# A product that nobody reads, issued before each chunk's sum in the message passes and in the attention pass

## The reference, cut to what matters

```
src, dst = edge_index                       # 31875 edges, sorted by dst
def _gine(x, ...):                          # called 4 times
    e = edge_attr @ eW + eb
    m = relu(x[src] + e)
    agg = segment_sum(m, dst, num_segments=N)
    h = (1.0 + eps) * x + agg
    return relu(h @ W1 + b1) @ W2 + b2
...
# attention: h_src = h_all[edge_type, src]
w = exp(leaky(scores) - amax[dst])
msg = h_src * (w / denom[dst])
out = segment_sum(msg, dst, num_segments=n)
```

## Time and profile before

| | us |
|---|---|
| median of 3 runs | 4661.29 (4660.78 to 4661.66) |
| the profiled execution | 4685.71 |
| its span, first to last instruction | 4684.1 |
| gathers of the first message pass, first to last issue | 180.1 to 567.7 |
| gathers of the second | 653.1 to 1043.0 |
| gathers of the third | 1131.0 to 1518.7 |
| gathers of the fourth | 1605.7 to 1993.6 |
| gathers of the attention pass | 2709.7 to 3092.9 |

### The profile page before, as it was taken

How to read it: one execution, slowest core, us unless ns; L and a number is a source line. 1 busy time by engine, 2 the same in 40 slices (tenths; PEclk the granted TensorE clock), 3 DMA queues, 4 the chain that set the end, 5 groups by cost and what they waited for, 6 DMA issues and landing times. The chain is left out here.

```text
span 4684.1 us, 57224 instructions
## 1 busy us (share of the span) xinstructions
PE 2923.7 (62%) x16851; PEld 2401.0 (51%) x16852; DVE 2212.2 (47%) x5663; ACT 867.9 (19%) x2228; POOL 1871.3 (40%) x1982
## 2 busy tenths in 40 slices
PE   3566746664666566642568626665949639947392
PEld 3455535553555355522556413335938639936382
DVE  6655645554555555564243437681064421134113
ACT  1122312221222122210112100001300103310020
POOL 4366546664666466624323467731010020020212
PEclk7788878777887778875678657676979859978696
DMA  6633323332333233303312133315947449945594
GB/s 157 217 89 89 78 65 89 88 83 59 89 90 88 57 87 89 89 15 124 100 55 74 28 82 93 92 41 190 304 145 240 150 159 328 325 150 174 181 333 128
DMA packets 357397, 598.97 MB, mean 128 GB/s; under 512 B 81862, under 2 KB 239864, under 8 KB 354808
## 3 DMA queue, kind: packets, MB, share of 16 engines
q1 hardware_dynamic: 245816, 357.76, 23.3%
q0 software_dynamic: 88640, 214.25, 16.3%
q10 hardware_dynamic: 22656, 23.54, 1.5%
HBM read 499.63 MB, written 95.75 MB: 127 GB/s over the span
## 5 line engine op out<-in xcount | busy, mean ns | idle before, releaser
L833 POOL DMA_INDIRECT gine_got<-gine_table,src x1056 | 1024.5, 970 | 619.7 <-issue 251.1
L893 PE MATMUL gine_p_sum<-gine_hot,gine_got 128*128 128x128 f32 x4224 | 846.2, 334 | 565.1 <-DVE stack_acc L930 200.1
L893 PEld LDWEIGHTS gine_p_sum<-gine_hot,gine_got 128*128 128x128 f32 x4224 | 707.4, 238 | 719.0 <-issue 648.6
L922 DVE TENSOR_TENSOR gine_got<-gine_got,gine_p_edge 128x256 f32<-128x256 f32 x1056 | 440.2, 418 | 633.5 <-PE gine_p_edge L884 365.0
L901 ACT ACTIVATE gine_got<-gine_got 128x256 f32<-128x256 f32 x1056 | 439.0, 417 | 1201.1 <-issue 750.5
L488 POOL DMA_INDIRECT adjacency<-value,place x264 | 281.1, 1065 | 475.9 <-POOLq L54 166.2
L930 DVE TENSOR_TENSOR stack_acc<-stack_acc,gine_p_sum 128x256 f32 x1056 | 438.9, 416 | 3.5 <-issue 0.7
L883 PE MATMUL gine_p_edge<-gine_w_a,edge_space 128*128 128x256 bf16 x1056 | 338.3, 320 | 42.6 <-issue 34.7
L1368 PE MATMUL ffn_p_h<-ffn_xt,ffn_w 128*128 128x128 f32 x2864 | 347.3, 279 | 1.1 <-DMA ffn_w<-in_L_ffn_w 0.7
L1368 PEld LDWEIGHTS ffn_p_h<-ffn_xt,ffn_w 128*128 128x128 f32 x2864 | 337.3, 196 | 3.8 <-DMA ffn_w<-in_L_ffn_w 2.6
L884 PE MATMUL gine_p_edge<-gine_w_b,edge_space 128*128 128x256 bf16 x1056 | 336.8, 319 | 0.0
(11 more groups left out here) (398 smaller groups left out, 3526.2 us busy)
## 6 DMA issues: line engine op xcount, KB each, us to landing
gcn_a<-adjacency SPq DMA_DIRECT2D x270, 320.0 KB
ffn_w<-in_L_ffn_W SPq DMA_DIRECT2D x74, 1024.0 KB
ffn_w<-in_L_ffn_w SPq DMA_DIRECT2D x60, 1024.0 KB
ffn_w<-in_L_ffn_w SPq DMA_DIRECT2D x90, 512.0 KB
adjacency<-zero_row ACTq DMA_DIRECT2D x3, 7200.0 KB, 43.8
gine_got<-gine_table,src POOLq DMA_INDIRECT x1056
h_table<-score_rows SPq DMA_DIRECT2D x15, 1056.0 KB
adjacency<-zero_row SPq DMA_DIRECT2D x1, 7200.0 KB, 28.1
```

Of the source, the lines that this page charges most:

```text
L833: pool.indirect_dma_start(got[:, c % RING, :], None, table, bass.IndirectOffsetOnAxis(ap=rows[:, c:c + 1], axis=0)).then_inc(gathered[c % ...
L893: ins = nc.tensor.matmul(p_sum[d % 4][:, half * P:(half + 1) * P], got[:, d % RING, half * P:(half + 1) * P], hot[:, d % HOTS, :], start=T ...
L922: nc.vector.tensor_tensor(got[:, c % RING, :], got[:, c % RING, :], p_edge[c % 4][:, 0:D], ALU.add).then_inc(summed, 1)
```

## The change

In both passes PE gets one more float32 product for each chunk, just before the wait for the chunk's message. Its stationary operand is the identity, its moving operand is a matrix that lies there anyway (`ew`, 256 columns) or is set to one once (`idle`, 240 columns), and it writes columns of the chunk's PSUM bank that no instruction reads (256 to 511, or 272 to 511). It signals nothing. In the message pass it stands behind the waits for `hot` and for the bank; in the attention pass behind the wait for the bank alone. DVE gets one memset and PE one wait for it at the start of the attention pass.

```
+def keep_running(nc, g, spare, moving):
+    nc.tensor.matmul(spare, g.ident[:, :], moving, start=True, stop=True)
...
                     if d >= 4:
                         pe.wait_ge(added, d - 3)
+                    keep_running(nc, g, p_sum[d % 4][:, D:2 * D], ew[:, :])
                     pe.wait_ge(msg_ready, d + 1)
...
-        shift = ph.sb("shift", [L, 2 * L])
+        shift, idle = ph.sb("shift", [L, 2 * L]), ph.sb("idle", [P, 240])
...
+        idle_made = ph.sem("idle_made")
...
+            pe.wait_ge(idle_made, 1)
             pe.wait_ge(shift_made, 1)
...
                     if c >= SUMS:
                         pe.wait_ge(added, c - SUMS + 1)
+                    keep_running(nc, g, p_sum[c % SUMS][:, 272:512], idle[:, :])
                     pe.wait_ge(hot_ready, c // G + 1)
                     pe.wait_ge(msg_ready, c + 1)
...
+            nc.vector.memset(idle[:, :], 1.0).then_inc(idle_made, 1)
             nc.vector.memset(shift[:, :], 0.0)
```

## The result

| | before | after |
|---|---|---|
| median of the timed runs, us | 4661.03 (4 runs, 4654.91 to 4661.66) | 4689.18 (4 runs, 4688.15 to 4696.61) |
| ratio to before | 1 | 1.0067, 95% interval 1.0049 to 1.0084 |
| the profiled execution's span | 4684.1 | 4686.7 |

What follows compares the result with a forecast made beforehand. The prediction took PE's late signals during gathers, not its computing, as the bound. It added 16 us for the message passes' ends, all else 0, to 4685.7, making 4702; the runs' median being 24.4 lower, 4677 us, range 4620 to 4720.

Steps and rivals of the forecast that it cites:

- the ends: After the last gather of each of four message passes, 21 new products lack cover: +16 us in all, bounds 0 and 37.
- What bounds the kernel: While POOL issues gathers, PE's signals reach the others 5 to 19 us late, and the passes go at their pace.
- The price of a product: On PE at 2.4 GHz, one new product costs 0.44 us, or 0.41 us with 240 columns.
- The gathers' stretches: Message passes while gathers are issued: the product lies in PE's waits or under the signals' lateness of 5 us: 0.
- the second rival: Message and attention passes: each of some 42 POOL stalls grows by 0.44 us, 18 us a pass; 4769 us, chance 0.12.
- The attention pass: Product hidden while gathers are issued; after the last, 18 us come out even against idle time and clock: 0, -5 to +7.
- The clock: In the five gather stretches, granted clock above 0.95 and PE busy above 75%; no time gain booked.
- The first rival: In stretches at 1.2 GHz others wait for PE, so a chunk takes 13% less; 4582 us in full, chance 0.20.
- the half case: The clock's gain decides in only half of the stretches at 1.2 GHz: 4635 us.
- The third rival: All hidden: the passes' ends have enough slack or the clock gives it back; 4661 us, 4652 to 4670, chance 0.24.

Runs made afterwards that it cites:

- e12: Changed kernel with 44, 24, 12 and 24 gather buffers in its message passes, product only in the fourth and in the attention pass; 0.9997 of the kernel before, third chip.
- e8: Kernel before without the product, PE signalling once for two chunks instead of once for each in the message passes; 0.9984 of the kernel before, second chip.
- e11: Kernel before with two new products for each chunk of the message passes, none in the attention pass; 4618.49 against 4361.17 us, ratio 1.0588, third chip.
- e1_before: Kernel before again, no edit, for a second profile on the first chip; 0.9999 of the kernel before.
- e4: Changed kernel without the new product for the last 22 chunks of each message pass, attention pass keeping it; 1.0058 of the kernel before, first chip.
- e6: Kernel before with the new product only for the last 22 chunks of each message pass, none in the attention pass; 1.0054 of the kernel before, second chip.
- e2: Kernel before with the new product in the four message passes alone; 4694.73 against 4663.18 us, ratio 1.0067, first chip.
- e7: Kernel before with a bf16 product, a quarter of the work, in the message passes and none in the attention pass; 1.0039 of the kernel before, second chip.
- e3: Kernel before with the new product in the attention pass alone; 4668.70 against 4663.18 us, ratio 1.0014, first chip.
- both ring runs: Kernel before with 44 and with 12 gather buffers instead of 24 in the message passes; 1.0006 and 0.9993 of the kernel before, third chip.
- e9: Kernel before with 44 gather buffers instead of 24 in the message passes; 1.0006 of the kernel before, third chip.
- e5: Changed kernel again, no edit, on the second chip; 1.0097 of the kernel before.

## Why the prediction was right, and where it was not

The time, the sign and the range held: 28 us slower against 16 forecast. Part of that is luck. Of the 28 us the sum had one term, the ends, and had booked the other at nothing; and the runs fell on the first chip. On the second the same change costs 43 us, and on the third, to judge by e12, next to nothing.

**What bounds the kernel: half right.** That PE's signals reach the others late while POOL issues gathers, and promptly when it has stopped, stands: e8 shows three engines idle with finished work, and the third chip shows the kernel without the lateness and 300 us faster. The lateness is a matter of some 4 us in most places; the 19 us of the earlier trace rows are from the start of a pass, which no experiment looked at further. Wrong is that "the passes go at the pace of those signals" in the sense of their number: half as many left the stretches as long. The lateness was also taken for a property of the kernel; it is one of the kernel on two of the three chips.

**The price of a product: right.** 0.44 us from product to sum in after's timeline; 1.10 us a chunk in the ends; twice 0.44 in e11.

**The ends: right.** Forecast +4.7, +4.2, +4.4, +3.4. Measured against the earlier trace rows +4.5, +3.4, +2.4, +3.1, and against e1_before, on the first chip, 17.5 us for the four. 16 us had been taken. e4 and e6 switch the term off and on. It has one condition that the prediction took for given: a backlog of some 22 chunks. On the third chip 5 are left, and there is no cost.

**The gathers' stretches: the term that was mis-sized.** "I take 0", with the argument that a lateness of 5 us covers 0.44. Measured: 2.7 to 4 us a pass on the first chip (after, e2, e4), 5.9 on the second, 0 on the third; 11 to 24 us in all where it counts, as much as the ends. What the argument missed is only in part shown: the product does not lengthen the stalls, which the cover of 5 us was meant against; with it POOL's bursts are of four or five gathers instead of mostly six, and its stalls shorter and more numerous (176 cycles to 218 on the first chip, 210 to 229 on the second), at a small loss. How the product brings that about stays open. The bound given for it, the second rival's 18 us a pass, was in the right direction and three to seven times too high (with 1.80 less 0.30 taken as 1.5 and not 1.4 it is 39 stalls and 17 us; 46 cycles a pass were counted in that profile), and e7 speaks against its rule: the cost does not go in proportion to the product's length. The profile that the sum was made from also hid it: its stretches of 388 us were, by all signs, those of another chip, beside which after's 387.5 look like nothing.

**The attention pass: nearly right.** Forecast 0 between -5 and +7, measured 5.5 us (2 to 11 by the interval) in e3. The forecast's own terms for the end (18 less 11.6 less 10) make -3.6 and not 0; the end did get 2.1 us shorter in e3, and 4 to 5 in after, but the stretch 3.9 us longer.

**The clock: right in the message passes, and worth nothing there.** 0.96 and PE busy for 76%, as forecast; in the attention pass 0.84 and 66%, where over 0.95 and 75% had been forecast. The first rival is refuted: with the clock up and PE's idle time filled, no stretch of a message pass got shorter than e1's. (Its price for the half case has a slip: half of 95 us is 47, which gives 4630 us and not 4635.) The Trainium skill's page "TensorE: Matmul & The Clock Gate", section "Why this matters for your kernels", asks to leave no idle gaps between bursts of products. As a rule on the clock the traces agree with it, 0.79 to 0.96; as a gain in time they do not, since e2 pays 31.5 us and e12's fourth pass gets nothing.

**All hidden: right on the third chip.** The third rival is what e12 shows there for the message passes. Which case holds is decided by the chip, a possibility that had no chance in the prediction.

**What stays open.** Why signals are late on two chips and not on the third, and what exactly releases them, no run shows. The traces hold one hint: on the first two chips many of the semaphore events are missing from the record (of the 1056 that tell of DVE's additions, 643 to 881 are there), on the third none is. Every timed execution was recorded as well (each has its span and clock on record), so it is not excluded that the recording has a part in the lateness. It is also not shown whether a ring of 12 buffers, with a shorter backlog and so shorter ends, would gain on a chip with late signals: both ring runs fell on the third. Why the product shortens the bursts is open too. The one variant that beat the kernel before is e8, by 8 us (0.16%, 0.07 to 0.25 by the interval).

## What to carry to other kernels

Before filling an engine's waits to raise its clock, ask who waits for that engine and whether it is late because it computes or because its signal travels: in the second case a faster engine buys nothing, and the filler costs wherever a backlog is worked off (0.44 us a chunk here, 9 us a pass, of which idle time and the clock gave back 5). A term booked at zero because "the wait covers it" deserves a bound from the cycle that makes the wait, not only from its length. And compare profiles from the same chip, or put both variants into one execution: here two chips differ by 20 us and a third by 300, with one and the same kernel, and the same change costs 28, 43 or next to 0 us.

## What the runs showed of the hardware

- **One kernel, three speeds.** 4663, 4683 and 4361 us on three chips. The granted clock is not the cause: after has 0.96 in the stretches of the first chip, as e9 and e12 have on the third without a product (0.96 to 0.98), and takes 387 us there against their 340. Nine tenths of the 300 us lie in the passes in which POOL issues indirect DMAs one after another.
- **Late signals.** On the first two chips a PE result reaches DVE and POOL late while gathers are issued, in e5 and e8 nearly always in a pause of POOL: 4.9 us after the sum in e8, 5.9 us in the earlier trace rows. DVE's signal to ACT is there in 0.03 us in the same stretches. From a gather's issue to its use it is 28.3 us in e1_before against 2.9 us on the third chip, though the data land after 2.4 us on both. The Trainium skill's page "Perfetto Trace Analysis", section "Tensor Engine Instruction (MATMUL, LD_WEIGHTS)", says that PE's recorded end is an estimate and that the signal goes out only after PSUM has acknowledged the write, so a record's end is no proof that the signal is out; it names no delay of microseconds. On the third chip the two agree to 0.04 us.
- **The gathers' own pace is the same everywhere**: 1.25 us from start to start, 0.95 of it busy, on all three chips.
